# A first layer norm on rows turned by the host, its mean and deviation spread by DMA, in a one-core attention and expert kernel

## What is computed

```python
mod = (_silu(L0_c) @ L0_wmod).reshape(L0_c.shape[0], 6, 1, -1)
sa, ca, ga, sb, cb, gb = (mod[:, 0], mod[:, 1], mod[:, 2], mod[:, 3], mod[:, 4], mod[:, 5])
...
h = _layernorm(x, axis=-1) * (1 + ca) + sa
x = x + ga * _L0_attn_ref(h, L0_attn_w_qkv, L0_attn_b_qkv, L0_attn_w_out, L0_attn_b_out)
h = _layernorm(x, axis=-1) * (1 + cb) + sb
x = x + gb * _L0_ffn_ref(h, L0_ffn_gate_W, L0_ffn_expert_W, L0_ffn_out_W)
```

## Time and profile before

| | us |
|---|---|
| median of three runs | 1567.94 |
| the three runs | 1562.91 to 1567.96 |
| span of the profiled execution, first to last instruction | 1560.2 |
| PE busy | 1472.0 (94%) |
| DVE busy | 1277.9 (82%) |
| ACT busy | 1147.2 (74%) |
| POOL busy | 858.0 (55%) |

### The profile page before, as it was taken

How to read it: one execution, slowest core, us unless ns; L and a number is a source line. 1 busy time by engine, 2 the same in 40 slices (tenths; PEclk the granted TensorE clock), 3 DMA queues, 4 the chain that set the end, 5 groups by cost and what they waited for, 6 DMA issues and landing times.

```text
span 1560.2 us, 56229 instructions
## 1 busy us (share of the span) xinstructions
PE 1472.0 (94%) x21476; PEld 946.3 (61%) x21476; DVE 1277.9 (82%) x3030; ACT 1147.2 (74%) x2464; POOL 858.0 (55%) x924
## 2 busy tenths in 40 slices
...
GB/s 170 99 150 127 171 156 173 152 170 157 149 178 155 175 153 166 143 168 167 157 180 152 160 146 170 166 160 157 165 142 167 175 150 178 154 169 139 157 73 50
DMA packets 197298, 239.73 MB, mean 154 GB/s; under 512 B 22462, under 2 KB 147782, under 8 KB 197030
## 3 DMA queue, kind: packets, MB, share of 16 engines
...
q10 hardware_dynamic: 64, 0.07, 0.0%
...
## 4 chain that ended last, share of the span: by engine, by line
PE 62%; DVE 10%; DMA 9%; issue 6%; SPq 6%; ACT 3%; POOL 2%; POOLq 0%; DVEq 0%; ACTq 0%
PE ps L599 26%; PE ps L753 11%; PE ps L748 8%; PE ps L807 6%; DMA qk_d<-qk_st 5%; PE ps L802 5%; DVE mxp L1089 3%; DMA kz<-qk_d 2%; PE ps L768 2%; PE ps L662 2%; SPq L412 2%; DVE ve_c L1014 1%; DVE zr L1101 1%; DVE st_c L1000 1%; SPq L429 1%
## 5 line engine op out<-in xcount | busy, mean ns | idle before, releaser
L1089 DVE TENSOR_REDUCE mxp<-ps 128x4 f32<-128x512 f32 (+1 forms) x1536 | 842.8, 592 | 160.5 <-PE ps L768 155.6
L863 ACT ACTIVATE prob<-ps 128x512 f32<-128x512 f32 (+1 forms) x1536 | 732.6, 525 | 121.8 <-PE ps L753 116.4
L753 PE MATMUL ps<-qs,kz 50*128 50x128 f16 (+2 forms) x3584 | 405.9, 240 | 12.9 <-DVE mxp L1089 10.5
L768 PE MATMUL ps<-kz,qs 49*128 49x128 f16 (+1 forms) x4096 | 410.5, 231 | 0.1
L753 PEld LDWEIGHTS ps<-qs,kz 50*128 50x128 f16 x3584 | 261.4, 94 | 88.7 <-ACT prob L863 31.1
L768 PEld LDWEIGHTS ps<-kz,qs 49*128 49x128 f16 x4096 | 286.3, 95 | 3.8 <-DVE mxp L1089 1.8
L1347 POOL TENSOR_TENSOR om<-oc,rz 128x512 f32<-128x512 f32 x62 | 77.4, 1270 | 329.9 <-DMA rz<-rz_d 329.9
L807 PE MATMUL ps<-prob,va 128*32 128x384 f32 (+2 forms) x3072 | 237.6, 381 | 0.0
L748 PE MATMUL ps<-mk 64*128 64x256 bf16 x1024 | 198.6, 274 | 36.0 <-DMA kz<-qk_d 11.3
L802 PE MATMUL ps<-prob,va 128*32 128x128 f32 x4096 | 209.6, 277 | 0.6 <-DVE qk_st L1021 0.6
L764 PE MATMUL ps<-mk 64*128 64x256 bf16 x1024 | 201.0, 276 | 5.4 <-DVE mxp L1089 3.4
...
## 6 DMA issues: line engine op xcount, KB each, us to landing
qk_d<-qk_st SPq DMA_DIRECT2D x128, 256.0 KB, 2.8
...
qs<-qk_d SPq DMA_DIRECT2D x256, 96.0 KB, 2.4
kz<-qk_d SPq DMA_DIRECT2D x256, 96.0 KB, 2.5
xa<-in_L_attn_x SPq DMA_DIRECT2D x32, 512.0 KB, 5.2
qk_d<-qk_st SPq DMA_DIRECT2D x128, 128.0 KB, 3.4
xc<-in_L_attn_x SPq DMA_DIRECT2D x32, 512.0 KB, 4.1
oc<-ou_d SPq DMA_DIRECT2D x31, 512.0 KB, 4.9
```

Source lines behind the costliest of these rows:

```text
L753: x_ = mm(bank[:, col:col + w * P], kz[rows, h // 2, kt * P:(kt + 1) * P], qs[rows, h // 2, qt * P:(qt + w) * P], start=(n > 0), stop=(n > ...
L768: x_ = mm(bank[:, col * P:(col + w) * P], qs[rows, h // 2, qt * P:(qt + 1) * P], kz[rows, h // 2, kt * P:(kt + w) * P], start=(n > 0), sto ...
L863: nc.scalar.activation(prob[:, h % 8, at:at + w], ps[:, ST + n, 0:w], ACT.Exp, scale=1.0 / FS).then_inc(s["exp_done"], 1)
L1089: v.tensor_reduce(mxp[:, g % 2, at, first:first + apart * (BLOCKS[n] - 1) + 1:apart], bank.rearrange("p (m k) -> p m k", k=P), AX.X, ALU.m ...
```

## The change

The host hands in x a second time as `x_turned`, with rows and columns swapped (256 x 512 per batch). It is loaded as `xt_a`, 128 partitions x 2 x 512. Mean and deviation are still made from `xa` by DVE, one row per partition. They are put side by side in `mr_a` (128 x 8), stored to DRAM (`store_mr`) and loaded back into all partitions (`load_mr`, `mr_bc`, 512 KB). POOL then norms the turned rows in four operations of 128 x 512 with two inputs in SBUF, add and multiply, and ACT applies scale and shift from SBUF. PE's `ta` and its eight transposes per batch are gone. For batch 0 the store and the load stand on ACT's queue.

```diff
 PE_AT = {
-    0: [(0, "out", 0, -2), (3, "ta", 0, 1)],
+    0: [(0, "out", 0, -2)],
...
 DVE_AT = {
...
-    7: [(3, "bn_a", 0, 2), (3, "bn_a", 1, 2), (3, "rmax", 3, 0)],
+    7: [(1, "bn_a", 2, 2), (3, "bn_a", 3, 2), (3, "rmax", 3, 0)],
...
+            def load_t(b, _):
+                wait(sp, "xna_ready", b * DC)
+                sp.dma_start(xt_a[:], x_turned[b].rearrange("(c p) t -> p c t", p=P)).then_inc(s["xt_loaded"], 16)
+
+            def store_mr(b, _):
+                wait(sp, "rsa_ready", b + 1)
+                wait(sp, "mr_loaded", b * 16)
+                sp.dma_start(mr_d, mr_a[:]).then_inc(s["mr_stored"], 16)
+
+            def load_mr(b, _):
+                wait(sp, "mr_stored", (b + 1) * 16)
+                wait(sp, "xna_ready", b * DC)
+                src = mr_d.rearrange("(o p) k -> o (p k)", o=1).broadcast_to([P, P * 2 * QT])
+                sp.dma_start(mr_bc[:].rearrange("p a k t -> p (a k t)"), src).then_inc(s["mr_loaded"], 16)
+
             def load_a(b, _):
-                wait(sp, "xna_ready", b * QT)
+                wait(sp, "lna_stats", b * QT)
                 sp.dma_start(xa[:], x[b].rearrange("(t p) d -> p t d", p=P)).then_inc(s["xa_loaded"], 16)
...
-            def ta(b, n):
-                dst = to("ta", n, b)
-                wait(pe, "xna_ready", (b + 1) * QT)
-                for t in range(QT):
-                    x_ = nc.tensor.transpose(dst[:, t * P:(t + 1) * P], xn_a[:, t, n * P:(n + 1) * P], ident[:])
-                x_.then_inc(s["ta_ready"], 1)
...
+            act.wait_ge(s["rsa_ready"], 1)
+            act.dma_start(mr_d, mr_a[:]).then_inc(s["mr_stored"], 16)
+            act.wait_ge(s["mr_stored"], 16)
+            act.dma_start(mr_bc[:].rearrange("p a k t -> p (a k t)"),
+                          mr_d.rearrange("(o p) k -> o (p k)", o=1).broadcast_to([P, P * 2 * QT])).then_inc(s["mr_loaded"], 16)
...
+            def hf_a_(b, n):
+                wait(act, "xna_ready", b * DC + n + 1)
+                wait(act, "hla_ready", b * 2)
+                nc.scalar.activation(hf_a[:, n, :], xn_t[:, n, :], ACT.Identity, bias=modT[:, b, 2 + n:3 + n],
+                                     scale=modT[:, b, n:n + 1]).then_inc(s["hfa_ready"], 1)
...
+            def rs_a_(b, _):
+
+                wait(pool, "lna_ready", (b + 1) * 2)
+                wait(pool, "mr_stored", b * 16)
+                q.tensor_tensor(rs_a, ve_a[:], neg_half[:], ALU.pow).then_inc(s["rsa_ready"], 1)
+
+            def norm_a(b, _):
+
+                wait(pool, "mr_loaded", (b + 1) * 16)
+                wait(pool, "xt_loaded", (b + 1) * 16)
+                wait(pool, "hfa_ready", b * 2)
+                wait(pool, "hha_ready", b * 2)
+                for c in range(DC):
+                    x_ = xt_a[:, c, :].rearrange("p (t a) -> p t a", t=QT)
+                    q.tensor_tensor(x_, x_, mr_bc[:, :, 0, :].rearrange("p a t -> p t a"), ALU.add).then_inc(s["xs_ready"], 1)
+                for c in range(DC):
+                    wait(pool, "xs_ready", b * DC + c + 1)
+                    q.tensor_tensor(xn_t[:, c, :].rearrange("p (t a) -> p t a", t=QT),
+                                    xt_a[:, c, :].rearrange("p (t a) -> p t a", t=QT),
+                                    mr_bc[:, :, 1, :].rearrange("p a t -> p t a"), ALU.mult).then_inc(s["xna_ready"], 1)
```

More of the change, by code:

```diff
@@ L173, in build @@
         ve_a = sb("ve_a", [P, QT], F32)
-        nm_a = sb("nm_a", [P, QT], F32)
-        rs_a = sb("rs_a", [P, QT], F32)
+        mr_a = sb("mr_a", [P, 2 * QT], F32)
+        nm_a, rs_a = mr_a[:, 0:QT], mr_a[:, QT:2 * QT]
+        mr_bc = sb("mr_bc", [P, P, 2, QT], F32)
+        xt_a = sb("xt_a", [P, DC, S], F32)
         hf_a = sb("hf_a", [P, DC, S], F32)
@@ L194, in build @@
         x1_last, x1_pre = xn_a, xa
+        xn_t = xn_a[:].rearrange("p (c u) d -> p c (u d)", c=DC)
         sel = rz[0:HALF].rearrange("p c t -> p (c t)")
@@ L322, in iterations @@
                 drain()
-        early = ("load_a", "bn_a", "ag_a", "norm_a")
+        early = ("load_a", "load_t", "store_mr", "load_mr", "bn_a", "ag_a", "rs_a", "norm_a")
         def play(i, t, table, steps, part=None, late={}):
@@ L379, in _ @@
             sp.dma_start(xa[:], x[0].rearrange("(t p) d -> p t d", p=P)).then_inc(s["xa_loaded"], 16)
+            sp.dma_start(xt_a[:], x_turned[0].rearrange("(c p) t -> p c t", p=P)).then_inc(s["xt_loaded"], 16)
             wm = wmod.rearrange("(k p) n -> p k n", p=P)
@@ L817, in qk_first @@
                     turn_weights()
-            steps = dict(ta=ta, t2=t2, qk=qk_first, v=v_, mt=mt, out=out_, gate=gate, moe=moe, pv=weigh)
+            steps = dict(t2=t2, qk=qk_first, v=v_, mt=mt, out=out_, gate=gate, moe=moe, pv=weigh)
             def drain():
@@ L1001, in stats, with aggregate @@
                 return one_tile
-            def aggregate(st, mv, ve, nm, names, norm, rs):
+            def aggregate(st, mv, ve, nm, names, norm, per, rs):
                 s_st, s_ag, s_rdy = names
                 def whole(b, _):
-                    wait(dve, norm, b * QT)
+                    wait(dve, norm, b * per)
                     wait(dve, s_st, (b + 1) * QT)
@@ L1103, in _ @@
             steps = dict(
-                bn_a=stats(xa, st_a, "xa_loaded", 16, "lna_stats", "xna_ready"),
+                bn_a=stats(xa, st_a, "xa_loaded", 16, "lna_stats", "lna_aggr"),
                 bn_c=stats(x1, st_c, "x1_ready", 2, "lnc_stats", "xnc_ready"),
-                ag_a=aggregate(st_a, mv_a, ve_a, nm_a, ("lna_stats", "lna_aggr", "lna_ready"), "xna_ready", "rsa_ready"),
-                ag_c=aggregate(st_c, mv_c, ve_c, nm_c, ("lnc_stats", "lnc_aggr", "lnc_ready"), "xnc_ready", "rsc_ready"),
+                ag_a=aggregate(st_a, mv_a, ve_a, nm_a, ("lna_stats", "lna_aggr", "lna_ready"), "mr_stored", 16, "rsa_ready"),
+                ag_c=aggregate(st_c, mv_c, ve_c, nm_c[:], ("lnc_stats", "lnc_aggr", "lnc_ready"), "xnc_ready", QT, "rsc_ready"),
                 qk_lo=qk_lo, ot=ot_, zs=zs_, gate_max=gate_max, gate_rest=gate_rest, gate_sum=gate_sum, gate_p=gate_p,
@@ L1366, in residual @@
                 if b == PRE:
-                    wait(pool, "xna_ready", NB * QT)
+                    wait(pool, "lna_stats", NB * QT)
                 else:
```

42 lines of the change are left out of this document (25 added, 17 removed), and 2 rows, old and new, of the table PE_AT.

## The result

| | before | with the change |
|---|---|---|
| median of the runs, us | 1566.55 (4 runs) | 1760.32 (4 runs, 1747.26 to 1767.52) |
| ratio, 95% interval | | 1.1237 (1.1188 to 1.1287) |
| span of the profiled execution, us | 1560.2 | 1763.5 |

The change makes the kernel 194 us slower. I had forecast 1673 us with a range of 1620 to 1730, so the direction was right and the size was wrong: the loss is nearly twice what my sum gave.

What follows compares the result with a forecast made beforehand. The loop from `zr` over SP's stores and loads to `kz` was taken to bound slot 8. 29 x (3.0 + 0.6 - 0.2) plus 7 gave 105.6 us, a span of 1666; with 7.7 on top 1673 us, range 1620 to 1730.

Steps and rivals of the forecast that it cites:

- What bounds it: Slot 4 to slot 8: the loop from `zr` over SP's stores and loads to `kz` sets slot 8's beginning; additions count in full.
- What the transposes are worth: PE's slots 0 and 2: removing transposes gains 0.2 us per iteration, bounds 0 and 1.03, as DVE is full there.
- What the two loads ahead of the q and k stores cost: SP's queue: `xa` and `xt_a` ahead of the stores make slot 8 later by 3.0 us per iteration.
- What the early statistics cost: DVE's `bn_a` in slot 5 waits 3.3 us (2.9 to 4.7) for `xa`; nothing is added to the loads' 3.0.
- my own formula: Slot 8's start by DVE's wait: 763.9, less PE's old wait of 1.2, plus DVE's wait of 3.3, gives 766.0.
- the two delays: Slot 8 comes at 766.0 by DVE's wait or 766.9 by the loads; only the longer counts, 3.0 us.
- if DMA lateness hits more than one place: Leftover case, such as `om` and the loads for slot 12: worse than 1725 us, chance 0.07.
- What the round trip of mean and deviation costs: POOL's norm after `mr_a`'s store and load: operations of 5.1 to 7.0 us make `x1` late, 0.6 us per iteration.
- The first rival: POOL much later: operations of 1.75 us, `x1` 1.9 us late, 4.7 us per iteration, 1711 us; chance 0.2.
- Start and end: Batch 0's norm makes the first q product 7 us later, once; the end is unchanged.
- the 7.7 us that I put on top: Median of the runs (1567.9) over the profiled span (1560.2), added to the forecast span of 1666 to give 1673 us.
- slot 8's `kz` and `negm` still end PE's wait: Sign expected in the profile if right: in slot 8 PE still waits for these loads, with `qk_d<-qk_st` landing about 3 us later.

Runs made afterwards that it cites:

- a_both: The changed kernel with both loads an iteration ahead in SP's slot 1, `load_t` ahead of the fourth stack load; 1643.4 us, 1.0505 of the kernel before.
- b_turns: The kernel before with one f16 product of constants in place of each group of four transposes; 1556.5 us, 0.9937 of the kernel before.
- b_xahalf: The kernel before with `load_a` ahead of the q and k stores, fetching only half of the rows (256 KB); 1593.5 us, 1.0187 of the kernel before.
- a_behind: The changed kernel with both loads behind the first two q and k stores, statistics still in slot 5; 1830.7 us, 1.1685 of the kernel before.
- a_early: The changed kernel with `load_a` an iteration ahead in SP's slot 1 and `load_t` behind the first stores; 1596.7 us, 1.0212 of the kernel before.
- b_bn5: The kernel before with only the change's DVE rows for `bn_a` and `ag_a` (slots 5, 7 and 9); 1797.8 us, 1.1497 of the kernel before.
- a_warm: The changed kernel with 36 unused products of constants on PE in slot 6, where PE waits for DVE; 1727.5 us, 1.1014 of the kernel before.
- a_bn7: The changed kernel with `bn_a` back in slots 7 and 8, both loads still ahead of the stores; 1733.6 us, 1.1069 of the kernel before.
- a_contig: a_early with POOL's reads of `mr_bc` contiguous instead of in steps of 32 bytes; 1575.0 us, 1.0043 of the kernel before.

## Why the prediction was wrong

**What bounds it: right for this loop.** Where only a load ahead of the stores is added, a microsecond more from `zr` to `load_stack` is about one in the period: 1.21 gives 1.1, 2.14 gives 2.1, 2.24 gives 2.5, 2.56 gives 3.1, 4.35 gives 4.8. It is not the only loop over DMA: a_both adds 0.3 there and 1.7 to the period, and in it `zr` itself comes late.

**"What the transposes are worth", 0.2 us: about right, as far as shown.** b_turns has 0.3 (0.1 by the period) for 0.6 of the 1.03 us. Most of what PE saves is lost again; that DVE's pace is what takes it back was argued from the earlier trace rows and not tested alone.

**"What the two loads ahead of the q and k stores cost", 3.0 us: mis-sized, 4.8.** I put the loads at the 323 GB/s of a stretch of mostly stores. Ahead of the stores 512 KB cost 2.14 to 2.56 us and 1 MB 4.35, a price of 205 to 245 GB/s, and b_xahalf shows that this is by the byte. Two things were wrong in it. That "transfers move in the order of issue, and `xa`, then last, holds up nobody" does not hold strictly: about half of `xa` moved before the stores had landed. And the engines do not stay full with the load ahead (table above); why they do not stays open, but the size of the pieces is not the main reason. The clock, which falls behind PE's wait for `negm`, is in the 4.8 as well.

**"What the early statistics cost", "the longer counts: still 3.0 us": this is the step that failed.** The mechanism and its place were right, and DVE's wait is 4.6 us, at the end of my bounds (2.9 to 4.7), because `xa` takes 5.6 us to land in the median, as the earlier trace rows had it, and not the 4.1 of `xc` that I took. But I then ran slot 8 from the end of the wait with nothing in between. By my own formula 4.6 us of wait give 763.9 - 1.2 + 4.6 = 767.3, 3.4 us of delay. In the trace PE comes back to a clock of 1.2 GHz and loses 2.7 us more on average, 2.15 in the iteration shown, which gives 6.1 against 5.9 measured (52.49 - 46.61). No term of my sum has the clock in it, since in the kernel before it is 1.00 all through the stretch that I read. With their own clock loss behind the wait added, 2.7 and 3.0, the formula also gives the two kernels in which only the wait is left: 6.8 - 1.2 + 2.7 = 8.3 for a_behind, which has the 0.65 us of a_early's period on top, 8.9 (measured 8.8), and 6.4 - 1.2 + 3.0 = 8.2 for b_bn5 (7.9). a_warm confirms 1.7 us of this term by a run; the rest is read from the traces.

That the two delays lie beside each other was right: alone the loads cost 4.8 us (a_bn7), the wait of 4.6 us alone about 6 by the formula (no run has a wait of that length alone), and together they cost 4.8 + 1.1 = 5.9. They are no sum. But it was the wait that counted, not the loads: PE does not wait for `negm` or `kz` at all between 400 and 1400 us. I gave 0.07 to a time over 1725 us, "if DMA lateness hits more than one place"; the time lies there, but for this other reason.

**"What the round trip of mean and deviation costs", 0.6 us: right.** Four operations take 6.1 us in the mean (5.1 to 7.0), and reading without steps gives back 0.7 us per iteration, with which the period of a_contig is that of the kernel before. The first rival, POOL much later, is refuted: an operation takes 1.53 us, not 1.75, and `x1` is idle only 0.17 us for `res`. (The Trainium skill's rule, GPSIMD Engine Reference, Performance pitfalls for Q7 kernels, half as much again, gave an estimate of 1.9 us. These runs have 1.53 against 1.27, which is 20% more: the effect is there, and in this operation, with one of two inputs in steps, it is smaller.)

**"Start and end", 7 us: mis-sized, 11.0.** The small store and the spread load took 5.0 and 5.8 us, POOL's operations 1.56 each. The 7.7 us that I put on top of the span were too many as well: time and span of one execution differ by 1.8 us in the changed kernel (1765.34 and 1763.5) and by 2.5 at the most in the others, so the 7.7 came from comparing different executions.

| term, us per iteration | predicted | measured | from |
|---|---|---|---|
| loads ahead | 3.0 | 4.8 | a_bn7 - a_early |
| wait for `xa` beside them | 0 | 1.1 | change - a_bn7 |
| POOL's steps | 0.6 | 0.7 | a_early - a_contig |
| transposes | -0.2 | -0.3 | b_turns (0.6 of the 1.03 us) |
| rest | 0 | 0.2 | |
| sum | 3.4 | 6.5 | |
| start, once | 7 | 11.0 | |

29 x 6.5 + 11 = 200 us, against 203 between the two spans. The clock has a share in the first two rows: at least 1.7 us together (a_warm). Of the signs that I named, DVE's wait in 29 iterations (4.6 us, not 3), PE's share under 90%, POOL's 1.53 us and the vanished idle time came true; the iterations are 52.5 us and not 49, the median landing of `qk_d<-qk_st` grew by 1.1 us and not by 3 (it has both pairs of stores in it, and `load_stack` comes 3.8 us later); "slot 8's `kz` and `negm` still end PE's wait" did not, and that it did not is what shows that the other of the two delays was the longer.
